# Down products of two batches by block sums, and two forget gate products in fp32

## The reference

```python
x = x + layernorm(mixer(layernorm(x)))
x = x + layernorm(ffn(layernorm(x)))
# mixer: i, f, g = x Wi^T, x Wf^T, x Wg^T; gate = sigmoid(f)
#        o_t = gate_t * o_(t-1) + silu(i_t) * (1 - gate_t)   (a scan over tokens)
#        (rms(o) * gnorm * silu(g)) Wo
# ffn:   hidden = silu(x W1^T) * (x W3^T)
#        out = fwht(hidden) W2^T                              (Hadamard transform of width 2048)
```

## Time and profile before

| | us |
|---|---|
| median of 3 runs | 683.46 (681.97 to 683.85) |
| profiled execution, its own time | 684.75 |
| span of the profile, first to last instruction | 683.0 |
| PE busy | 657.3 |
| VectorE (DVE) busy | 409.6 |
| ScalarE (ACT) busy | 352.5 |
| GpSimd (POOL) busy | 236.3 |
| mean granted TensorE clock | 0.995 |

### The profile page before, as it was taken

How to read it: one execution, slowest core, us unless ns; L and a number is a source line. 1 busy time by engine, 2 the same in 40 slices (tenths; PEclk the granted TensorE clock), 3 DMA queues, 4 the chain that set the end, 5 groups by cost and what they waited for, 6 DMA issues and landing times.

```text
span 683.0 us, 11543 instructions
## 1 busy us (share of the span) xinstructions
PE 657.3 (96%) x4340; PEld 425.9 (62%) x4340; DVE 409.6 (60%) x791; ACT 352.5 (52%) x629; POOL 236.3 (35%) x216
## 2 busy tenths in 40 slices
PE   3898999999999999999989999999999999999996
PEld 2444344444465677777767777668777777777762
DVE  6989899999999999983546412144212113521224
ACT  4999876372675766554534434335333343533231
POOL 1237467674752244165225212122211111311121
PEclk9999999999999999999999999999999999999999
DMA  8992543107344474983995224596434232742002
GB/s 334 407 403 95 124 124 62 62 1 186 116 155 147 170 268 147 321 308 129 198 329 198 109 108 172 101 267 232 145 129 159 95 123 108 261 187 79 31 1 92
DMA packets 60743, 114.12 MB, mean 167 GB/s; under 512 B 40464, under 2 KB 40720, under 8 KB 56080
## 3 DMA queue, kind: packets, MB, share of 16 engines
q1 hardware_dynamic: 60688, 113.39, 49.8%
HBM read 80.87 MB, written 23.07 MB: 152 GB/s over the span
## 4 chain that ended last, share of the span: by engine, by line
PE 61%; DVE 11%; issue 3%; SPq 2%; DVEq 2%; DMA 2%; ACT 1%; POOL 0%; POOLq 0%
PE ps L635 20%; PE ps L637 20%; PE ps L636 20%; SPq L611 2%; DVEq L1052 2%; DMA out<-res 1%; DVE o_s L1142 1%; DVE st L1051 1%; DVE w2t L1306 1%; DVE ring L1193 1%; DVE x1r L1306 1%; DMA res<-x_rows 1%; DVE ps L1137 1%; DVE ring L1251 1%; DVE mv L1053 1%
## 5 line engine op out<-in xcount | busy, mean ns | idle before, releaser
L635 PE MATMUL ps<-xb,ring 128*128 128x256 f16 (+1 forms) x704 | 212.7, 302 | 6.5 <-ACT ps L961 3.2
L637 PE MATMUL ps<-xb,ring 128*128 128x256 f16 (+1 forms) x704 | 212.7, 302 | 0.0
L636 PE MATMUL ps<-xb,ring 128*128 128x256 f16 (+1 forms) x704 | 212.7, 302 | 0.0
L1421 POOL TENSOR_TENSOR ring<-sga,ring 128x512 f16<-128x512 f32 x64 | 78.1, 1224 | 304.8 <-ACT ring L1007 304.6
L635 PE MATMUL ps<-ring 128*128 128x256 f16 x384 | 105.2, 274 | 0.0
L636 PE MATMUL ps<-ring 128*128 128x256 f16 x384 | 105.0, 274 | 0.0
L637 PE MATMUL ps<-ring 128*128 128x256 f16 x384 | 105.0, 273 | 0.0
L635 PE MATMUL ps<-w2t,ring 128*128 128x512 f16 x256 | 97.4, 380 | 0.0
L637 PE MATMUL ps<-w2t,ring 128*128 128x512 f16 x256 | 97.4, 380 | 0.0
L636 PE MATMUL ps<-w2t,ring 128*128 128x512 f16 x256 | 97.4, 380 | 0.0
L635 PEld LDWEIGHTS ps<-xb,ring 128*128 128x128 f16 x704 | 69.0, 98 | 45.2 <-ACT ps L961 4.3
(11 more groups left out here) (165 smaller groups left out, 1034.1 us busy)
## 6 DMA issues: line engine op xcount, KB each, us to landing
ring<-w_comb SPq DMA_DIRECT2D x24, 1792.0 KB, 7.7
ring<-W13t SPq DMA_DIRECT2D x14, 1024.0 KB, 12.4
w_comb<-ring SPq DMA_DIRECT2D x8, 1792.0 KB, 6.7
rows<-L_attn_hidden_states SPq DMA_DIRECT2D x16, 256.0 KB, 4.2
w2t<-W2t SPq DMA_DIRECT2D x8, 512.0 KB, 12.2
res<-L_attn_hidden_states SPq DMA_DIRECT2D x16, 256.0 KB, 4.3
x_rows<-res SPq DMA_DIRECT2D x16, 256.0 KB, 3.2
x1r<-x_rows SPq DMA_DIRECT2D x16, 256.0 KB, 3.4
```

Of the source, the lines that this page charges most:

```text
L635: pe.matmul(dst, a_hi, b_hi, start=start, stop=False, skip_group_check=onto)
L636: pe.matmul(dst, a_hi, b_lo, start=False, stop=False, skip_group_check=onto)
L637: return pe.matmul(dst, a_lo, b_hi, start=False, stop=stop, skip_group_check=onto)
L1421: pool.tensor_tensor(hid(b, c, 1), sga[:, c % 2], hid(b, c, 0), ALU.subtract).then_inc(hid_lo, 1)
```

## The change

- **Down products of batches 2 and 3.** A unit (p, j) takes two token tiles and two hidden chunks; W2's width of 512 is two halves. Seven block products (Winograd's form) of three passes with 256 columns replace eight. A batch has 16 units, the first eight with p = 0 (tiles 0, 1). Sums of hidden blocks (SU, four VectorE operations of 128 columns a chunk) are split by a second ScalarE and a second GpSimd operation. Sums of W2 blocks are made once: TA, TL (VectorE) and TW (ScalarE) in batches 0 and 1, TB, TM and TC in batches 1 and 2. EV adds the seven results into `res`, from which V and W now read. In the last batch the last four units of p = 1 run product by product (DT).
- **Ring.** The units and sums take ring space, so batches 1 to 3 use two slots for combined weights.
- **Forget gate.** F.0.0 and F.0.1 multiply the raw fp32 weights with raw fp32 x (`x_raw`, a further ScalarE copy of each of the four transposes of batch 0). `x_raw` and the raw weights lie where UL.6, UL.7 and NL.5 load, which now wait for F.0.1. Chunks 2 and 3 of Wf are split first.
- **Orders.** All five lists are written anew; bank numbers change. The hidden scale's exponent goes from 15 to 13 and W2's from 5 to 6.

```diff
+FFN_EXP = 13
+W2_LESS = 6
+EVEN_UNITS = (52, 55.5, 8, 11.5, 15, 18.5, 22, 25.5)
+ODD_UNITS = (59, 62.5)
+COMBINED_SLOTS = 2
+END_UNITS = 4
+FIRST_UNITS = 2
+END_PRODUCTS = (1, 5, 2, 6, 7, 3, 4)
 MIXER_OF = (1, 2, 3, 0)
+RAW_FORGET = 2
...
+D.1.56 GP.2.2:7 D.1.57 D.1.58 D.1.59 GQ.2.2:5 GU.2.1 GR.2.2 GP.2.3:6 D.1.60 D.1.61 D.1.62 GU.2.2 GQ.2.3:4 D.1.63
+GP.2.4:7 GR.2.3 GQ.2.4:5 GU.2.3 GR.2.4 GP.2.5:6 GU.2.4 GQ.2.5:4 D.2.0 GR.2.5 GP.2.6:7 D.2.1 GU.2.5 GP.2.7:6 GQ.2.6:5
+GQ.2.7:4 GR.2.6 GR.2.7 GU.2.6 GU.2.7 GP.2.8:7 GP.2.9:6 D.2.2 GQ.2.8:5 GQ.2.9:4 GR.2.8 GR.2.9 GU.2.8 GP.2.10:7 D.2.3
...
+GP.3.1:6 GQ.3.0:5 D.2.6 GQ.3.1:4 GR.3.0 GR.3.1 GP.3.2:7 GU.3.0 GP.3.3:6 GU.3.1 GQ.3.2:5 D.2.7 GQ.3.3:4 GR.3.2 GR.3.3
+GU.3.2 GP.3.4:7 GU.3.3 GP.3.5:6 D.2.8 D.2.9 D.2.10 D.2.11 D.2.12 GQ.3.4:5 D.2.13 GR.3.4 D.2.14 GQ.3.5:4 GU.3.4
+GP.3.6:7 GR.3.5 D.2.15 GQ.3.6:5 GU.3.5 GP.3.7:6 GR.3.6 D.3.0 D.3.1 GQ.3.7:4 GU.3.6 GP.3.8:7 GR.3.7 D.3.2 GU.3.7
...
+GP.3.15:6 GQ.3.14:5 GQ.3.15:4 GR.3.14 GR.3.15 GU.3.14 GU.3.15 D.3.6 D.3.7 D.3.8 D.3.9 D.3.10 D.3.11 DT.3.0 DT.3.1
+DT.3.2 DT.3.3 DT.3.4 DT.3.5 DT.3.6
...
+SU.2.14 SU.2.15 GR.3.0 GU.3.0 GR.3.1 GU.3.1 UP.3.0 SU.3.0 UP.3.1 SU.3.1 EV.2.0 GR.3.2 GU.3.2 V.2.0 GR.3.3 GU.3.3 V.2.1
...
+UP.3.13 SU.3.13 GR.3.14 GU.3.14 GR.3.15 GU.3.15 UP.3.14 SU.3.14 UP.3.15 SU.3.15 EV.3.0 V.3.0 V.3.1 W.3.0 W.3.1 EV.3.1
+V.3.2 V.3.3 W.3.2 W.3.3
...
+ZD.2.5 ZD.2.6 LR.0.2 O.0.0 LR.0.3 O.0.1 LZ.3.0 LZ.3.1 LR.1.0 O.0.2 LZ.3.2 LR.1.1 O.0.3 WL.1.3 LZ.3.3 WL.1.4 WL.1.5
...
-            return (HC // 2 * f + j) % SLOTS
+            return j % SLOTS if f == 0 else j % COMBINED_SLOTS
...
+        def unit_step(f, at):
+
+            if f < B - 1:
+                return divmod(at, HC // 2)
+            steps = [(0, j) for j in range(7)] + [(1, 0), (1, 1), (1, 2), (0, 7), (1, 3)]
+            return steps[at]
+
...
+                if m >= UNITS - 2:
+                    sp.wait_ge(f_mm, RAW_FORGET)
...
+                if j == 5:
+                    sp.wait_ge(f_mm, RAW_FORGET)
...
-                last = n - SLOTS
+                last = n - COMBINED_SLOTS
                 if last < HC // 2:
                     sp.wait_ge(st_s[last % SLOTS], 16 * (last // SLOTS + 1))
                 sp.wait_ge(up_mm, 2 * last + 2)
-                sp.dma_start(slot(f, j), w_comb[j]).then_inc(ld_wc[n % SLOTS], 16)
+                sp.dma_start(slot(f, j), w_comb[j]).then_inc(ld_wc[j % COMBINED_SLOTS], 16)
...
+            def raw_forget(b, c):
+                pe.wait_ge(xt_raw, TC)
+                pe.wait_ge(ld_aw[0], 16)
+                wait_bank("F", b, c)
+                for k in range(KC):
+                    last = pe.matmul(bank("F", b, c)[:], att_raw(0)[:, k, chunk(c)], x_raw[:, k, :],
+                                     start=k == 0, stop=k == KC - 1)
+                last.then_inc(f_mm, 1)
...
-                    pe.wait_ge(ld_wc[n % SLOTS], 16 * ((n - HC // 2) // SLOTS + 1))
+                    pe.wait_ge(ld_wc[j % COMBINED_SLOTS], 16 * ((n - HC // 2) // COMBINED_SLOTS + 1))
...
+            def down_product(f, p, j, q, start):
+                block = {1: 0, 2: 2, 3: 6, 4: 3, 5: 1, 6: 4, 7: 5}[q]
+                right = {1: 11, 2: 21, 3: 22}
+                spot, half = {1: (0, 0), 5: (0, 1), 2: (1, 0), 6: (1, 1), 7: (2, 0), 3: (2, 1), 4: (3, 0)}[q]
+                w_hi, w_lo = (w2_block(right[q], j, part) if q < 4 else w2_sum({5: 1, 6: 2, 7: 3, 4: 4}[q], j, part)
+                              for part in range(2))
+                dst = sums_bank(f, p, spot)[:, 256 * half:256 * (half + 1)].rearrange("p (u d) -> p u d", d=UW)
+                return three_passes(dst, unit_block(f, p, j, block, 0), unit_block(f, p, j, block, 1), w_hi, w_lo,
+                                    start, False, True)
+            def down_unit(f, at):
+                p, j = unit_step(f, at)
+                n = HC * f + 2 * j + 2 - p
+                pe.wait_ge(hid_hi, n)
+                pe.wait_ge(hid_lo, n)
+                if f == FIRST_UNITS and p == 0:
+                    pe.wait_ge(tw_lo, 3 * j + 3)
+                    pe.wait_ge(tb_lo, j + 1)
+                if j == 0:
+                    if f == FIRST_UNITS and p == 0:
+                        pe.wait_ge(v_norm, TC * f)
+                    elif f == B - 1 and p == 1:
+                        pe.wait_ge(hid_rdy, HC * B)
+                        pe.wait_ge(c12_rdy, HC * B)
+                    else:
+                        pe.wait_ge(ev_rdy, 14 * (f - FIRST_UNITS) + 7 * p)
+                for q in (1, 5, 2, 6, 7, 3, 4):
+                    last = down_product(f, p, j, q, j == 0 and q in (1, 2, 7, 4))
+                last.then_inc(du_mm, 1)
+            def down_end(f, i):
+                if i == 0:
+                    pe.wait_ge(hid_hi, HC * (f + 1))
+                    pe.wait_ge(hid_lo, HC * (f + 1))
+                for j in range(HC // 2 - END_UNITS, HC // 2):
+                    last = down_product(f, 1, j, END_PRODUCTS[i], False)
+                last.then_inc(dt_mm, 1)
...
+                if b == 0:
+                    act.activation(x_raw[:, :, chunk(t)], quarters(bank("XT", b, t)), ACT.Copy).then_inc(xt_raw, 1)
...
+            def split_unit(f, c):
+                act.wait_ge(su_rdy, 4 * (HC * (f - FIRST_UNITS) + c + 1))
+                number, units = unit_number(f, c), ODD_UNITS if c % 2 else EVEN_UNITS
+                if number >= len(units):
+                    act.wait_ge(du_mm, unit_done(number - len(units), c % 2))
+                elif number < 2:
+                    act.wait_ge(up_mm, 12)
+                    act.wait_ge(st_s[2], 32)
+                else:
+                    act.wait_ge(d_mm, HC * FIRST_UNITS)
+                to = unit_at(f, c, 0)
+                act.activation(to[:, 0:512], sga[:, c % 2], ACT.Copy).then_inc(hid_mid, 1)
+                act.activation(to[:, 512:896], hidden_sums(c), ACT.Copy).then_inc(hid_hi, 1)
...
+            def copy_p1(f, p):
+                if f == B - 1 and p == 1:
+                    act.wait_ge(dt_mm, 2)
+                else:
+                    act.wait_ge(du_mm, units_done(f, p))
+                if f > FIRST_UNITS or p > 0:
+                    act.wait_ge(ev_rdy, 14 * (f - FIRST_UNITS) + 7 * p)
+                else:
+                    act.wait_ge(tb_lo, HC // 2)
+                act.activation(temp(0), sums_bank(f, p, 0)[:, 0:256], ACT.Copy).then_inc(a1_rdy, 1)
...
+            def hidden_unit_sums(f, c):
+                n = HC * (f - FIRST_UNITS) + c
+                dve.wait_ge(hid_rdy, HC * f + c + 1)
+                h = [sga[:, c % 2, chunk(i)] for i in range(4)]
+                s = [hidden_sums(c)[:, chunk(i)] for i in range(3)]
+                if n == 0:
+                    dve.wait_ge(y_mm, TC * B)
+                dve.tensor_tensor(s[1], h[0], h[1], ALU.subtract).then_inc(su_rdy, 1)
+                dve.wait_ge(su_rdy, 4 * n + 1)
+                dve.tensor_tensor(h[1], h[1], h[3], ALU.add).then_inc(su_rdy, 1)
+                dve.wait_ge(su_rdy, 4 * n + 2)
+                dve.tensor_tensor(s[0], h[1], h[0], ALU.subtract).then_inc(su_rdy, 1)
+                dve.wait_ge(su_rdy, 4 * n + 3)
+                dve.tensor_tensor(s[2], h[2], s[0], ALU.subtract).then_inc(su_rdy, 1)
...
+            def down_results(f, p):
+                n, end = 14 * (f - FIRST_UNITS) + 7 * p, f == B - 1 and p == 1
+                to = [res[:, 2 * p + i, 256 * k:256 * (k + 1)] for i in range(2) for k in range(2)]
+                p1, u2, u3, u4 = (temp(i) for i in range(4))
+                def products(count):
+                    if end:
+                        dve.wait_ge(dt_mm, count)
+                if not end:
+                    dve.wait_ge(du_mm, units_done(f, p))
+                dve.wait_ge(a1_rdy, 2 * (f - FIRST_UNITS) + p + 1)
+                for i in range(2):
+                    dve.wait_ge(st_out[2 * p + i], 16 * f)
+                products(4)
+                dve.tensor_tensor(to[0], sums_bank(f, p, 1)[:, 0:256], p1, ALU.add).then_inc(ev_rdy, 1)
+                dve.tensor_tensor(u2, sums_bank(f, p, 1)[:, 256:512], p1, ALU.add).then_inc(ev_rdy, 1)
+                dve.wait_ge(ev_rdy, n + 2)
+                dve.tensor_tensor(u4, sums_bank(f, p, 0)[:, 256:512], u2, ALU.add).then_inc(ev_rdy, 1)
+                products(6)
+                dve.wait_ge(ev_rdy, n + 3)
+                dve.tensor_tensor(to[1], sums_bank(f, p, 2)[:, 256:512], u4, ALU.add).then_inc(ev_rdy, 1)
+                dve.tensor_tensor(u3, sums_bank(f, p, 2)[:, 0:256], u2, ALU.add).then_inc(ev_rdy, 1)
+                dve.wait_ge(ev_rdy, n + 5)
+                dve.tensor_tensor(to[3], sums_bank(f, p, 0)[:, 256:512], u3, ALU.add).then_inc(ev_rdy, 1)
+                products(7)
+                dve.tensor_tensor(to[2], u3, sums_bank(f, p, 3)[:, 0:256], ALU.subtract).then_inc(ev_rdy, 1)
             def v(b, t):
-                if t < TC - 1:
+                if b >= FIRST_UNITS:
```

(9 more changed lines are left out.)

388 lines of the change are left out of this document (234 added, 154 removed).

## The result

The changed kernel takes 692.73 us (median of 4 runs, 688.28 to 695.56) against 683.63 for the kernel before on the same chip: a ratio of 1.0119, interval 1.0091 to 1.0147. It is **slower by 9 us**; the forecast was 675.9, faster, and the range ended at 682.0. The profiled execution took 695.56 us (span 693.8); on the scale of the sum the forecast was 677.1, so 18.4 us have to be found.

What follows compares the result with a forecast made beforehand. The prediction took TensorE's stream of products to bound the kernel (busy 657.3 of 683.0 us). Terms -9.4 + 1.0 + 2.0 + 0 - 3.0 + 1.8 = -7.6 us gave 677.1, or 675.9 as median; range 671.5 to 682.0.

Steps and rivals of the forecast that it cites:

- The prediction's own sign of being wrong: Prediction wrong if stalls in batches 2 and 3 exceed 8 us in sum, or the start loses more than 2.
- Part 1: Down products of batches 2 and 3: 256-column products at 0.109 us save 4.7 us a batch, 9.4 for two.
- Rival (d): Block products don't keep their pitch: 288 additional weight loads show, +28 us, 704; chance 0.03 with anything unnamed and slow.
- What the units need: Added sums and splits for the block products: mostly hidden, with thin cover on VectorE; +1.0 us (0 to 4).
- Part 2: Two slots for combined weights: pair loads wait for a later product, stalling batches' products; +2.0 us (0.3 to 10).
- three load waits that were named: TensorE waits for combined weight loads before GP.2.4, GP.2.6 and GP.3.10, named as what would show the two slots' price.
- Part 3: Forget gate at the start: fp32 products cost 1.7 us of TensorE, earlier start regains it; net 0 (-2 to +1.5).
- Part 4: TensorE's hole at 356 us in batch 1: new SyncE order brings the reload sooner, no half clock; -3.0 us (-4.7 to 0).
- the hole of 4.5: TensorE's wait near 356 us for a late reload of res, 2.91 us, with half clock behind; predicted as 4.7 in all.
- Part 5: Kernel's end: one addition and tile 2's statistics now follow the last product; +1.8 us (+0.4 to +2.5).
- (b): Rival: seeds queue behind splits in many pairs of batches 2 and 3, 5 us on top, 681; chance 0.09.
- (c): Rival: loads at pair heads in batches 2 and 3 decide; 684.3 at 9.0 us landing, 687.3 at 9.3; chance 0.12.

Runs made afterwards that it cites:

- Kernel 1: The changed kernel with SyncE's first loads back in the order of the kernel before; 692.11 us, ratio 1.0099.
- kernels 3: The changed kernel with all five engines' lists in the order of before through the mixer, and split forget weights instead of fp32 products; 703.47 us, ratio 1.0289.
- 4: The changed kernel with all lists in the order of before through the mixer, fp32 forget products kept; 707.35 us, ratio 1.0338.
- 6: Kernel 4 with the second half of each combined weight load left out; 698.45 us, ratio 1.0219.
- kernel 7: The kernel before's lists through batch 1's down products, W2 block sums inserted, three slots there; the changed kernel's lists after, split forget weights; 702.00 us, ratio 1.0254.
- 9: Kernel 7 with the fp32 forget products added; 706.21 us, ratio 1.0312.
- kernel 10: The kernel before's order to the end of batch 0's gate and up products, split forget weights; the changed kernel from there, two slots; 690.97 us, ratio 1.0099.
- 11: Kernel 10 with three slots for combined weights in batch 1 and three down steps moved between products with late seeds; 689.70 us, ratio 1.0084.
- kernel 12: Kernel 7 with W2's block sums cut to 4 columns for all pairs but the first; 684.53 us, ratio 1.0010.
- 14: Kernel 11 with steps of all five engines in batches 0 to 3 reordered from summed trace durations, and TA cut in two steps; 681.15 us, ratio 0.9950.
- 15: Kernel 11 with TA cut in two and a second order found from summed durations, from another start; 680.58 us, ratio 0.9944.
- 16: The kernel before with one pair load of combined weights moved later on SyncE, behind two reloads of res; 685.15 us, ratio 1.0011.
- 17: The kernel before with all four reloads of res ahead of that pair load on SyncE; 687.39 us, ratio 1.0049.
- kernel 18: Kernel 15 with further steps of the five engines moved, by summed durations from 15's own trace; 679.42 us, ratio 0.9935.
- kernel 5: The changed kernel with o's squares moved ahead of weight norm passes on ScalarE, and GpSimd's last addition of them moved earlier; 690.31 us, ratio 1.0100.
- kernel 2: The changed kernel without the fp32 forget products, using split weights as before; 693.85 us, ratio 1.0138.
- kernel 13: The changed kernel with W2's block sums cut to 4 columns for all pairs but the first; 690.77 us, ratio 1.0109.

## Why the prediction was wrong, point by point

**The failed step** is the one that isn't there. "Orders. All five lists are written anew" got no term of its own: I costed what the new lists hold, and where I looked at order (pair distances for the loads, EV.2.0, the reload) it was at the places of the new operations. For the mixer the prediction says "the same steps precede XT.1.3 in both orders", and stops there. From H2.0.0 on, ScalarE's squares, its norm passes and its weight splits stand in another order; in the profiled execution that cost 4.6 us up to F.1.3, 3.3 from GP.0.0 to D.0.0, 4.1 to GP.0.6 and 1.2 to GP.1.0, 13.2 in all where the prediction had nothing. Kernel 1, with the same lists but for SyncE's loads, loses 9.7 there; the rest are stretches at the lower clock that come in one execution and not in another. Wherever a kernel has the old lists in a stage, it has the old idle time there, with and without block products and fp32 products: 4.0 and 1.3 to 1.5 in the first two of these stages (kernels 3, 4, 6, 7, 9 to 12, 14 to 18), 0.2 to GP.0.6 (7, 9 to 12, 14 to 18) and 0.2 to GP.1.0 (7, 9, 12, 16, 17). That this is order is shown; which step it is at each wait is shown for MS.0.0 (kernel 5), read from ScalarE's list for D.0.1, and not followed for the others. The prediction's own sign of being wrong, a start or batches 2 and 3 that lose too much, looked at neither of these stages.

**Part 1, right.** Work fell by 7.7 with the fp32 products in it and by 9.4 without (643.7 against 653.1 in kernels 2 and 14). The last three products of the changed kernel:

```profile
685.98 0.27 PE L713 MATMUL ps<-ring 128*128 128x256 f16 x1
686.09 0.27 PE L714 MATMUL ps<-ring 128*128 128x256 f16 x1
686.20 0.27 PE L715 MATMUL ps<-ring 128*128 128x256 f16 x1
```

0.11 apart. The sign I had named, "PE busy down by about 9 us", was wrong: it didn't move, for the reason given above. Rival (d) falls. So does, for this kernel, the Trainium skill's 131 ns at 512 columns (TensorE: Matmul & The Clock Gate, Back-to-back issue gap): the kernel before shows 0.215 us there.

**What the units need, and Part 2: +3.0 predicted, 5.4 measured** for batches 2 and 3. Two of the three load waits that were named came, 3.1 us together against the 2.0 of Part 2:

```profile
477.31 0.28 PE L713 MATMUL ps<-xb,ring 128*128 128x256 f16 x1 [0.82 <-DMA ring<-w_comb]
...
493.30 0.28 PE L713 MATMUL ps<-xb,ring 128*128 128x256 f16 x1 [2.31 <-DMA ring<-w_comb]
```

These are GP.2.4 and GP.2.6. GP.3.10 did not wait, and GP.1.6, in batch 1, which wasn't named, did, 0.9 us. The loads land in 7.0 us at least, 7.5 in the median and 11.1 at most, as assumed. Most of the rest is lost at GU.2.4, GR.2.6 and GR.2.11, 0.6 to 0.7 us each, against the +1.0 for what the units need. The sentence "none of the engines is full there" was right for batches 2 and 3, VectorE 31.5 of 80 us:

```profile
400.00:480.00 80.00, 79.18 (x595) 57.55 (x594) 31.52 (x78) 33.13 (x68) 16.20 (x16) 1.00 0.47 148
```

and wrong for the W2 sums, which I put into one clause. They fall into batches 0 and 1, where the kernel before has VectorE at 9 tenths to slice 17; at EV.2.0 I had set 3.9 us of PE's cover against VectorE's queue, but the W2 sums I weighed as single operations of 0.42, not as a TA of 4.2. It cost the changed kernel little (kernel 13) only because its order was made for it, and 17.5 us where it wasn't (kernel 12 against 7).

**Part 3: its net of 0 held in the changed order** (kernel 2 against the changed kernel), with the start 1.6 better: F.0.0 starts at 14.69 us, as worked out, and the lead ends not at F.1.0, which starts at 58.14 (57.91 before; I had about 1 later), but in the 2.83 us that H2.0.0 waits just ahead of it. GpSimd's butterflies, which H2.0.0 waits for, came no sooner. The 1.7 us before WS.0.0 are gone, as hoped. In the old order the same products cost 3.9 and 4.2 us, more than the 1.7 of work: the start didn't give it back, and went from 5.1 to 5.8 and from 4.6 to 5.9. The price of a step depends on the order around it; mine was for neither.

**Part 4, half right.** No half clock: the clock in the window 320 to 400 is 1.00. But the named sign, no wait over 1 us at ScalarE's seed, failed: the hole of 4.5 became waits at GP.1.6, GR.1.6 (1.55 us behind ScalarE's L1107) and GR.1.7, 3.3 in all, and a new one of 1.1 stands at GQ.1.1. Batch 1's idle time went from 5.4 to 5.0, so -0.4 instead of -3.0. VectorE still sat for a reload, the last one, later:

```profile
377.04 0.69 DVE L1227 BATCH_NORM_STATS2 st<-res 128x6 f32<-128x512 f32 x1 [4.27 <-DMA res<-x_rows]
```

Its output's store lands at 370.37; the reload is issued at 370.39 and takes 6.6 us beside the pair load that SyncE had issued at 367.58, where the median of that line between 340 and 385 us is 3.0. Kernels 16 and 17 show the same for the kernel before: loads and reloads share the queues, and one of them is late.

**Part 5, right.** From the last product to the end of the span 7.3 us, against 5.8: +1.5. The last addition at 686.51, tile 2's statistics, then tile 3's at 688.08:

```profile
686.51 0.42 DVE L1594 TENSOR_TENSOR res<-ot,ps 128x256 f32<-128x256 f32 x1
686.85 0.69 DVE L1227 BATCH_NORM_STATS2 st<-res 128x6 f32<-128x512 f32 x1
...
688.08 0.68 DVE L1227 BATCH_NORM_STATS2 st<-res 128x6 f32<-128x512 f32 x1
```

**The rivals.** None of them gave slower by 9 us for the reason that held. (b) named the right mechanism, in-order queues with foreign steps ahead, for the wrong batches; (c) was the slower one and didn't decide. The chance of slower, 0.08, was 0.05 for the loads and 0.03 for (d) with anything unnamed; a rewritten order of 4 engines and a DMA queue should have been a rival with a price from rows: each wait it adds costs its length and, for some of those above 2 us, up to 1.7 more. The hole at 356 us was such a row.

## What to carry to other kernels

When a change rewrites the order of in-order queues, that is the change: walk the lists of every engine through the stages that compute nothing new, and give the order a term and a rival of its own. Compare the cover of a product (the work that PE has left before it needs the result) with the longest step that can stand ahead of its producer (4.2 us here), not with an instruction (0.42), and look at what stands behind a waiting load on the issuing queue as well as at who waits for the load. Saved work is worth its pitch only once its preparation is placed where it holds nothing up; here the lists decided between +2.5% (kernel 7) and -0.6% (kernel 18) for the same products. How much of the second is order alone is open, as said above.

## What the runs showed of the hardware

VectorE and GpSimd operations lengthen each other. In the changed kernel VectorE's L1370 takes 0.68 us when no GpSimd operation is under way at its start, and 1.76 when L1680 is. VectorE, then GpSimd:

```profile
378.10 0.68 DVE L1370 TENSOR_TENSOR gate<-rows,gate 128x512 f16<-128x512 f32 x1
...
381.59 1.76 DVE L1370 TENSOR_TENSOR si<-rows,si 128x512 f16<-128x512 f32 x1
```

```profile
381.26 1.53 POOL L1680 TENSOR_TENSOR res<-rows,res 128x512 f32<-128x512 f32 x1
```

The GpSimd operation ends at 382.79, and 0.68 later, 383.47, is about where VectorE's ends (383.35): as if it had waited for the whole of the other. The Trainium skill (SBUF — State Buffer, SBUF: two separate sides) says just that: the pair of ports shared by the two is an exclusive lock for the whole instruction, among others for VectorE operations with two inputs in SBUF against a GpSimd operation that reads SBUF, and the one that starts second waits. The trace agrees here. It goes the other way too: the GpSimd addition of 3.37 us ahead of MS.0.0 starts at 65.75, while a VectorE operation is under way; three more with two inputs follow on VectorE until 67.99, and the addition ends at 69.12, as if it had run only after them. In kernel 5, where it comes earlier, it takes 1.26 us. I had priced each of the new operations alone.

A wait of PE doesn't always cost clock. The three waits of 2.3 to 2.8 us shown first were each followed by a stretch at the lower level; those of 2.1 and 2.4 at the same places in kernels 1, 2 and 13 were not, and neither was the one of 2.31 us ahead of 493.30 in the same kernel:

```profile
493.00:500.00 7.00, 6.70 (x62) 6.01 (x63) 4.02 (x9) 3.09 (x7) 1.21 (x2) 1.00 0.26 51
```

What sets this apart is open.

One store of 256 KB to HBM took 9.1 us beside a load of 1792 KB (kernel 10), where the median of the same stores in the changed kernel is 2.6.
